# A third PSUM bank for the row maxima, and narrow matrix products packed side by side, in a two-layer attention and feed-forward kernel

## The chip, the core and the metric

The kernel runs on one core of a Trainium2 chip. The metric is the device time of one launch in microseconds (us). Three runs of the kernel before gave 6522.10, 6526.37 and 6527.11 us; their median is 6526.37 us. Engines are named as in the profile: PE is TensorE (PEld its weight loads), DVE VectorE, ACT ScalarE, POOL GpSimd, SP the queue that issues most of the DMAs.

## The reference

There are 16 batch elements of 512 tokens with 256 channels, and for each a context of 1601 tokens. Two layers follow each other:

```python
# layer 0
x = x + cross_attention_16_heads(layernorm(x), ctx)   # head size 16, q and k layer-normed per head, softmax over 1601
x = x + gelu_ffn(layernorm(x))                        # 256 -> 64 -> 1024 -> gelu -> 64 -> 256, low rank
# layer 1
x = x + one_head_attention(layernorm(x), ctx, mask)   # head size 16, scores normalised over the 1601 keys, softmax
x = x + soft_moe(layernorm(x))                        # 64 experts with 32 slots each; softmax over the batch and over the slots
```

The change touches everything up to the soft mixture of experts, which is stage two of the kernel and stays as it is.

## The kernel before

Stage one computes all but the experts. Its main loop runs over 16 batch elements and, in each, over 52 steps: 4 groups of 4 heads by 13 chunks of 128 keys (the last has 65). The step's own work on PE stands in a fixed order:

- four score products (`score_columns`, L789), one per head, into two PSUM banks in turn; ACT turns each into exponentials (L1038);
- four or five pieces of row maxima for the next group (`row_piece`, L767, 401 keys each), into two other banks in turn, the ring; DVE reduces each bank to its maximum (L1193). Transposed maxima and the finished heads (`maxima`, `heads_out`) take their turns in the same ring;
- the weighted values (`weigh_values`, L800): four products of 17 columns that write different 32-partition strips of one bank.

In a step the order is: score, piece, place 0, piece, score, piece, place 1, score, piece, place 2, score, piece, weighted values. At the three places stand the woven steps, which a table of positions (`woven`) spreads over the 52 steps: position 16.67 is place 2 of step 16. They belong to two chains. The head of the next batch element (T transposed input, K keys and values, Q queries, kv1 layer-one keys and values, X transposed heads) fills one bank, `hb`, again and again, and ACT empties it. The tail of the previous batch element fills two banks, `b6` and `b7`: attnT, proj, xT, u1, V1 (eight feed-forward chunks up), U2 (eight down), v2, q1, cq, qaT, s1 (13 score chunks of layer one), pv1, out. Each engine takes its instructions in its own written order and waits on semaphores; a woven step that waits holds up all that stands behind it on its engine. A product that reuses a bank waits until its reader is done (`m_free` for the ring, `h_free` for `hb`, `t_act` and `t_dve` for the tail's banks).

A product in fp32 shows as two MATMUL records. Three products are narrow: kv1 (L740) has 32 output rows, U2 (L842) has 64, and s1 (L903) has 32 rows of contraction that count, padded with zeros to 128. POOL normalises (L644 to L647) and applies the gelu parts (L657 to L665).

Of the kernel before, what the change touches and what calls it, by code (L numbers as in the profile page):

```python
# [12 lines left out]
P = 128  # L13
# [46 lines left out]
def woven():  # L60
# [40 lines left out]
    put(4.0, -1, "attnT", 0)  # L101
    put(4.34, -1, "attnT", 1)
    put(5.34, -1, "proj", 0)
    put(5.67, -1, "proj", 1)
    put(6.34, -1, "res", 1, 0)
    put(6.67, -1, "res", 1, 1)
    for t in range(QT):
        put((6.67, 7.0, 7.34, 7.67)[t], -1, "bns", 1, t)
        put((25.34, 25.7, 26.0, 26.34)[t], -1, "bns", 2, t)
        put((44.0, 44.34, 45.0, 45.34)[t], -1, "bns", 3, t)  # L110
    put(8.0, -1, "lnv", 1)
    put(8.01, -1, "lna", 1)
    put(8.02, -1, "base", 2)
    put(9.67, -1, "xT", 1, 0)
    put(10.0, -1, "xT", 1, 1)
    put(10.34, -1, "u1")
    for f in range(FC):
        put((11.0, 11.34, 11.67, 12.0, 15.9, 16.67, 17.67, 18.67)[f], -1, "V1", f)
        put((11.34, 11.67, 12.67, 13.67, 16.34, 17.34, 18.34, 19.34)[f], -1, "gpre", f)
        put((12.34, 13.34, 14.0, 14.67, 18.0, 19.0, 20.0, 21.0)[f], -1, "gtanh", f)  # L120
        put((12.35, 13.35, 14.01, 14.68, 18.01, 19.01, 20.01, 21.01)[f], -1, "gpost", f)
        put((15.67, 16.34, 17.34, 18.34, 20.0, 21.0, 22.0, 23.0)[f], -1, "U2", f)
    put(23.67, -1, "pT2")
    put(24.34, -1, "v2", 0)
    put(24.67, -1, "v2", 1)
    put(25.0, -1, "res", 2, 0)
    put(25.67, -1, "res", 2, 1)
    put(26.67, -1, "lnv", 2)
    put(26.68, -1, "lna", 2)
    put(26.69, -1, "base", 3)  # L130
    put(28.34, -1, "xT", 2, 0)
    put(28.67, -1, "xT", 2, 1)
    put(29.34, -1, "q1")
    put(0.34, -1, "km")
    put(0.7, -1, "kc")
    put(2.0, -1, "v1")
    put(2.5, -1, "v1e")
    put(3.0, -1, "cov")
    put(3.5, -1, "cove")
    put(30.0, -1, "cq")  # L140
    put(30.67, -1, "cqe")
    put(31.34, -1, "cs")
    put(32.0, -1, "cse")
    put(32.01, -1, "sgp")
    put(33.0, -1, "qs")
    put(33.67, -1, "qaT")
    put(34.34, -1, "q1a")
    for c in range(KC):
        put(35.0 + 0.5 * c, -1, "s1", c)
    for k in range(4):  # L150
        put((36.95, 38.95, 40.95, 41.95)[k], -1, "pv1", k)
    put(42.34, -1, "o1")
    for t in range(QT):
        put((43.0, 43.34, 44.0, 44.34)[t], -1, "out", t)
        put((43.67, 44.0, 44.67, 45.0)[t], -1, "res", 3, t)
    put(45.67, -1, "lnv", 3)
    put(45.68, -1, "lna", 3)
    put(47.67, -1, "xT", 3, 0)
    put(48.0, -1, "xT", 3, 1)
    put(49.0, -1, "st3")  # L160
# [15 lines left out]
    "pT2": ("t_act",), "q1": ("t_mm", "t_act"), "kc": ("kc_ready",), "km": ("km_ready",), "cov": ("t_mm",), "cove": ("t_dve",), "cq": ("t_mm",),  # L176
# [9 lines left out]
def landed(b, label, at):  # L186
# [8 lines left out]
    if name == "ldV":  # L195
        return [(f"va_loaded{label[1] % 2}", 16)]
    return [(n, v) for n, v in {"stV": [("v_stored", 16)], "stkv1": [("kv1_stored", 16)],
                                "ldX": [("xw_loaded", 16), ("kv1_loaded", 16)], "st3": [("x_stored", 48)]}.get(name, [])]


def counted():

    value, at = {}, {}
    for it in range(-2, B + 1):
        for s in range(STEPS):
            for place in WOVEN[s]:
                for of, label in place:
# [67 lines left out]
NLOAD = 17 + 2 * (P // HD) + 4 + 1  # L275
# [15 lines left out]
SETUP_DVE = 41  # L291
# [3 lines left out]
def stage_one(nc, x, ctx_d, mask, w, x3_d, xn_d, xnT_d, ident, psum):  # L295

    with ExitStack() as st:
# [3 lines left out]
        S_BANK, M_BANK, V_BANK, H_BANK, T_BANK = (0, 1), (2, 3), 4, 5, (6, 7)  # L301
# [4 lines left out]
        kv1_d = nc.dram_tensor("kv1_scratch", (B, 2 * A1, NK), F32, kind="Internal").ap()  # L306
# [7 lines left out]
        v2 = sb("v2", [RANK, D])  # L314
# [4 lines left out]
        bkv = sb("bkv", [2 * A1, 1])  # L319
# [22 lines left out]
        kv1s = sb("kv1s", [2 * A1, S])  # L342
# [25 lines left out]
        kmean = sb("kmean", [A1, 1])  # L368
        cov = sb("cov", [A1, A1])
        q1T = sb("q1T", [A1, S])  # L370
        qa = sb("qa", [P, QT, 2 * A1])
        ksum = sb("ksum", [2 * A1, 4, 4])
# [72 lines left out]
        def _(sp):  # L445
# [7 lines left out]
                (v2[:, :], w["L0_ffn_V2"]),  # L453
# [5 lines left out]
                (bkv[0:A1, :], w["L1_xattn_bk"].rearrange("(p a) -> p a", a=1)),  # L459
                (bkv[A1:2 * A1, :], w["L1_xattn_bv"].rearrange("(p a) -> p a", a=1)),  # L460
# [3 lines left out]
            ]  # L464
            for j in range(P // HD):
# [31 lines left out]
            def store_keys_one(b, i):  # L497
                n = min(S, NK - i * S)
                sp.wait_ge(h_free, at("h_free", b, "kv1", i))
                sp.dma_start(kv1_d[b][:, i * S:i * S + n], kv1s[:, 0:n]).then_inc(kv1_stored, 16)  # L500
# [36 lines left out]
            def load_tail(b):  # L537
# [3 lines left out]
                if b >= 1:  # L541
                    sp.wait_ge(h_full, at("h_full", b - 1, "s1", KC - 1))
# [141 lines left out]
        def _(pe):  # L684
# [1124 lines left out]
```

## Time and profile before

| | |
|---|---|
| median of 3 runs | 6526.37 us |
| profiled execution, its own time | 6520.53 us |
| its span | 6518.7 us |
| mean granted clock of TensorE | 0.971 |
| busy in the span: PE, DVE, ACT, POOL | 91%, 56%, 51%, 37% |
| stage one, from the start to the first product of stage two | 4666.78 us |
| main loop, batch elements 1 to 15 (478.08 to 4484 us) | 4005.92 us, 267.1 each |
| the last tail by itself (4484 to 4639 us) | 155 us |

The span goes from the first to the last profiled instruction. PE records are pipelined: the end of a record is modelled and lies after the time at which the next product may start, so the distance between the starts of two records, not their length, says what a product costs. A wait that is shorter than this overhang doesn't show as idle time of PE.

### The profile page before, as it was taken

The page shows a single profiled execution, that of the slowest core. Times are in us where ns is not written, and L with a number is a line of the kernel's source. Part 1 is how long each engine was busy: PE and PEld are TensorE (multiplying, and loading weights), DVE is VectorE, ACT ScalarE, POOL GpSimd, SP SyncE. Part 2 cuts the span into 40 slices and gives each one's busy share as a digit, 9 for nine tenths or more (in the row PEclk, how much of TensorE's full clock was granted, in tenths as well). Part 3 has the DMA queues.
Part 4 walks back from the last instruction along what each step waited for, and adds up shares of the span by engine and source line. Part 5 has one row for each costly group of instructions (what it writes and reads, how often), then busy time and mean ns, then how long its engine had stood idle before and what let it go on. Part 6 is the DMA issues. An engine that isn't in the chain of part 4 may idle for free. (4 is left out here: it accounts for less than half of the span.)

```text
span 6518.7 us, 93097 instructions
## 1 busy us (share of the span) xinstructions
PE 5927.6 (91%) x35613; PEld 2981.1 (46%) x35613; DVE 3677.9 (56%) x6989; ACT 3300.6 (51%) x6257; POOL 2407.3 (37%) x2686
## 2 busy tenths in 40 slices
PE   3789999999999999999999999997599999998999
PEld 1223333333333333333333333322388888886888
DVE  3565656656566565565665656661366666652333
ACT  1366666666666666666666666654222222223332
POOL 3226355363462634636346364443222222220000
PEclk9799999999999999999999999997799999999999
DMA  2441432414324143241332423310356666666553
GB/s 63 78 76 51 79 72 58 83 50 77 69 58 85 49 76 69 61 86 50 74 70 60 84 56 71 62 28 15 127 187 214 221 213 214 209 211 249 211 195 117
DMA packets 417819, 680.30 MB, mean 104 GB/s; under 512 B 61376, under 2 KB 316432, under 8 KB 415072
## 3 DMA queue, kind: packets, MB, share of 16 engines
q1 hardware_dynamic: 307552, 565.29, 34.0%
q10 hardware_dynamic: 109824, 109.07, 5.0%
q8 instruction: 282, 4.62, 0.3%
q14 instruction: 161, 1.32, 0.1%
HBM read 455.04 MB, written 218.39 MB: 103 GB/s over the span
## 5 line engine op out<-in xcount | busy, mean ns | idle before, releaser
L1193 DVE TENSOR_REDUCE mx<-psum 128x1 f32<-128x401 f32 x4096 | 2212.1, 570 | 1612.8 <-PE psum L767 1603.7
L1038 ACT ACTIVATE probs<-psum 128x512 f32<-128x512 f32 (+1 forms) x3328 | 1910.5, 599 | 906.6 <-PE psum L789 903.5
L767 PE MATMUL psum<-kst,qst 96*128 96x401 bf16 x4096 | 1354.9, 343 | 191.9 <-DVE mx L1193 150.9
L789 PE MATMUL psum<-qst,kst 99*128 99x512 bf16 (+1 forms) x3328 | 1284.5, 386 | 49.8 <-ACT probs L1038 44.8
L800 PE MATMUL psum<-probs,vaug 128*17 128x512 f32 x6656 | 885.8, 604 | 0.0
L789 PEld LDWEIGHTS psum<-qst,kst 99*128 99x128 bf16 (+1 forms) x3328 | 328.8, 99 | 1177.1 <-ACT probs L1038 750.4
L767 PEld LDWEIGHTS psum<-kst,qst 96*128 96x128 bf16 x4096 | 402.6, 98 | 961.4 <-DVE mx L1193 756.1
L1486 POOL TENSOR_TENSOR disp<-disp,rz 128x2048 f32<-128x2048 f32 x64 | 294.3, 4599 | 925.4 <-DVE rz L1716 925.4
L1505 PE MATMUL psum<-phi,xT 128*128 128x128 f32 x4096 | 512.2, 280 | 39.2 <-DMA xT<-xnT_scratch 31.9
L1520 PE MATMUL psum<-disp,xnb 128*128 128x128 f32 x4096 | 495.5, 280 | 49.9 <-DMA xnb<-xn_scratch 30.7
L1505 PEld LDWEIGHTS psum<-phi,xT 128*128 128x128 f32 x4096 | 480.4, 193 | 86.9 <-issue 79.2
L1520 PEld LDWEIGHTS psum<-disp,xnb 128*128 128x128 f32 x4096 | 479.9, 196 | 58.5 <-DMA xnb<-xn_scratch 31.1
L644 POOL TENSOR_SCALAR rs<-mv 128x4 f32<-128x4 f32 x48 | 11.1, 231 | 1242.4 <-DVE mv L1245 1242.4
L725 PE MATMUL psum<-wkv,cT 128*128 128x512 f32 (+1 forms) x832 | 406.6, 611 | 12.7 <-ACT sq L1006 7.2
L1749 DVE COPY disp<-psum 128x512 f32<-128x512 f32 x256 | 176.9, 691 | 366.4 <-PE psum L1562 366.3
L1574 PE MATMUL psum<-disp 128*128 128x256 f32 x1536 | 366.6, 380 | 4.6 <-DVE xnb L1766 2.5
L1595 ACT ACTIVATE disp<-psum 128x512 f32<-128x512 f32 x256 | 152.1, 597 | 430.6 <-PE psum L1505 430.3
L1621 ACT ACTIVATE xT<-xT,nm 128x512 f32<-128x512 f32 x256 | 181.0, 708 | 347.7 <-DMA xT<-logit_scratch 338.7
L1723 DVE TENSOR_TENSOR ysb<-psum,be 128x512 f32<-128x512 f32 x128 | 88.5, 691 | 461.7 <-PE psum L1535 450.3
L1627 ACT ACTIVATE slT<-psum 128x512 f32<-128x512 f32 x128 | 76.4, 597 | 435.9 <-PE psum L1520 435.9
L1574 PEld LDWEIGHTS psum<-disp 128*128 128x128 f32 x1536 | 276.0, 190 | 39.6 <-DVE xnb L1766 5.6
L1535 PE MATMUL psum<-we,slT 128*32 128x256 f32 x4096 | 248.6, 383 | 0.0
(190 smaller groups left out, 7527.2 us busy)
## 6 DMA issues: line engine op xcount, KB each, us to landing
xnb<-xn_scratch SPq DMA_DIRECT2D x256, 512.0 KB, 3.8
kst<-k_planes SPq DMA_DIRECT2D x384, 200.1 KB, 8.7
logit_scratch<-disp ACTq DMA_DIRECT2D x64, 1024.0 KB, 5.3
xT<-logit_scratch SPq DMA_DIRECT2D x32, 2048.0 KB, 8.3
k_planes<-pl SPq DMA_DIRECT2D x96, 384.0 KB, 3.2
y_scratch<-ysb ACTq DMA_DIRECT2D x128, 256.0 KB, 5.3
vaug<-v_scratch SPq DMA_DIRECT2D x64, 442.0 KB, 4.3
v_scratch<-vst SPq DMA_DIRECT2D x48, 544.0 KB, 3.1
```

The source lines that it names most:

```text
L725: last = mm(hb[0:m, :], cT[:, n % 2, k, a * P:a * P + m], wkv[:, k, :], start=(k == 0), stop=(k == 1))
L767: mm(to[:, 0:PW], qst[g][0:NP, j, t * P:(t + 1) * P], kst[g][0:NP, j, k0:k0 + PW], start=True, stop=True).then_inc(m_full, 1)
L789: mm(bank[S_BANK[n % 2]][0:m, :], kst[g][0:NR, j, c * P:c * P + m], qst[g][0:NR, j, :], start=True, stop=True).then_inc(s_full, 1)
L800: last = mm(bank[V_BANK][32 * j:32 * j + HV, :], vaug[0:m, g % 2, c, HV * j:HV * (j + 1)], probs[0:m, 4 * (k % 2) + j, :], start=(c == 0), ...
L1038: fn(probs[0:m, 4 * (k % 2) + j, :], bank[S_BANK[j % 2]][0:m, :], ACT.Exp, scale=float(HD) ** 0.5).then_inc(s_exp, 1)
L1193: v.tensor_reduce(mx[:, n % 2, u // 4, u % 4:u % 4 + 1], bank[M_BANK[r % 2]][:, 0:PW], AX.X, ALU.max).then_inc(m_free, 1)
L1486: pool.tensor_tensor(d, d, rz[:, n % 2, None, :].broadcast_to((P, B, SL)), ALU.mult).then_inc(normed, 1)
L1505: last = mm(bank[u % 4][:, a * SL:(a + 1) * SL], xT[:, 4 * q + a, k, t * P:(t + 1) * P], phi[:, k, s * SL:(s + 1) * SL], start=(k == 0), s ...
L1520: last = mm(bank[4 + n % 2][:, (2 * a + h) * SL:(2 * a + h + 1) * SL], xnb[:, a, t, h * P:(h + 1) * P], disp[:, (QT * s + t) % RING, b, :] ...
L1535: last = mm(bank[6 + n % 2][32 * j:32 * j + 32, a * D:(a + 1) * D], slT[:, n % 2, a, k, 32 * j:32 * j + 32], we[:, s % 2, j, k, :], start= ...
L1574: last = mm(bank[4 + t][:, a * D:(a + 1) * D], exT[n % 4][:, t * P:(t + 1) * P], ya[b % 4][:, e, :], start=(e == 0 and a == 0), stop=(e == ...
L1621: fn(d, d, ACT.Exp, bias=nm[:, t, b:b + 1], accum_out=sums[:, b % 4, t, h:h + 1]).then_inc(c_exp, 1)
```

## The change

- The ring of row maxima gets bank 7 as a third bank in steps 0 to 37 and 47 to 51 of every batch element (`LENT`). Each use takes the bank whose last use is the oldest. The order of pieces and scores in a step is as before.
- The tail keeps only bank 6, but for steps 38 to 46, where pv1 and out use bank 7 as before. Its two-bank steps become fill, empty, fill, empty, and their positions in the table move. V1 4 to 7 use `hb`, the bank of the head.
- U2: two chunks at once into the two halves of bank 6 (64 partitions each). The halves are added by v2, whose contraction is now 128 rows, with the weights twice below each other.
- kv1: the 512 tokens are cut in four, and the four products of 128 tokens write four 32-partition strips of `hb`. ACT reads 128 x 128 instead of 32 x 512. The keys' sums then lie in four strips, and a small product with `sel` (the new step km) adds them. The store and the load of `kv1T` are cut to match, and the load is made twice, into partitions 0 to 31 and 64 to 95 (four DMAs instead of one).
- s1: two chunks at once, one from rows 0 to 63 into `hb`, one from rows 64 to 127 into bank 6; the queries `q1a` lie twice, in rows 0 and 64. Seven steps instead of 13.
- There are 7 more loads of weights and 10 more set-up instructions on DVE.

```diff
-    put(4.0, -1, "attnT", 0)
-    put(4.34, -1, "attnT", 1)
+    put(3.0, -1, "attnT", 0)
+    put(3.67, -1, "attnT", 1)
...
-    put(47.67, -1, "xT", 3, 0)
-    put(48.0, -1, "xT", 3, 1)
+    put(49.34, -1, "xT", 3, 0)
+    put(50.0, -1, "xT", 3, 1)
...
+LENT = [s < 38 or s > 46 for s in range(STEPS)]
...
+        free = [m for m in (2, 3, 7) if m != 7 or (LENT[k % STEPS] and k < B * STEPS)]
+        home = min(free, key=lambda m: -1 if last[m] is None else last[m])
...
                 for k in range(2):
-                    last = mm(hb[0:2 * A1, 0:m], w1kv[:, k, :], cT[:, n % 2, k, 0:m], start=(k == 0), stop=(k == 1))
+                    for j in range(-(-m // P)):
+                        w = min(P, m - j * P)
+                        last = mm(hb[32 * j:32 * j + 32, 0:w], w1kv[:, k, :], cT[:, n % 2, k, j * P:j * P + w],
+                                  start=(k == 0), stop=(k == 1), skip_group_check=True)
...
             def ring_bank(use):
-                n = RING[use]
-                if n >= 2:
-                    pe.wait_ge(m_free, n - 1)
-                return bank[M_BANK[n % 2]]
+                home = HOMES[RING[use]]
+                if home[1] is not None:
+                    pe.wait_ge(m_free, home[1] + 1)
+                if len(home) == 3 and home[2] >= 0:
+                    pe.wait_ge(t_dve, at("t_dve", home[2], "res", 3, QT - 1))
+                return bank[home[0]]
...
             def project(b, i):
-                pe.wait_ge(t_act, at("t_act", b, "attnT", 1))
+                if i == 0:
+                    pe.wait_ge(t_act, at("t_act", b, "attnT", 1))
+                else:
+                    pe.wait_ge(t_dve, at("t_dve", b, "res", 1, 0))
...
             def ffn_up(b, f):
-                before = ("u1",) if f < 2 else ("V1", f - 2) if f < 5 else ("V1", f - 1)
-                pe.wait_ge(t_act, at("t_act", b, *before))
-                to = b7 if f in (1, 3) else b6
-                mm(to[:, :], v1[:, f * P:(f + 1) * P], pT[0:RANK, :], start=True, stop=True).then_inc(t_mm, 1)
...
+                if f < 4:
+                    pe.wait_ge(t_act, at("t_act", b, *(("V1", f - 1) if f else ("u1",))))
+                    to, signal = b6, t_mm
+                else:
+                    head_bank(b, "V1", f)
+                    to, signal = hb, h_full
+                mm(to, v1[:, f * P:(f + 1) * P], pT[0:RANK, :], start=True, stop=True).then_inc(signal, 1)
...
-                mm(b7[0:RANK, :], u2[:, f, :], hx[:, f % 4, :], start=(f == 0), stop=(f == FC - 1)).then_inc(t_mm, 1)
+                pe.wait_ge(g_post, at("g_post", b, "gpost", 2 * p + 1))
+                for a in range(2):
+                    last = mm(b6[RANK * a:RANK * a + RANK, :], u2[:, 2 * p + a, :], hx[:, (2 * p + a) % 4, :],
+                              start=(p == 0), stop=(p == FC // 2 - 1), skip_group_check=True)
+                last.then_inc(t_mm, 1)
...
+                mm(hb[0:m, :], kv1T[0:64, c * P:c * P + m], q1a[0:64, :], start=True, stop=True).then_inc(h_full, 1)
+                if c + 1 < KC:
+                    mm(b6[:, :], kv1T[64:P, (c + 1) * P:(c + 2) * P], q1a[64:P, :], start=True,
+                       stop=True).then_inc(t_mm, 1)
```

The row order on PE in steps 16 and 17 of a batch element, before. L842 is a U2 product, L748 the head's X, L836 a V1 product; L789 and L767 are scores and pieces, L800 the weighted values:

```order
L842 MATMUL psum<-hx,u 64x512
L748 MATMUL psum<-ident,kraw 128x128 x4
L789 MATMUL psum<-qst,kst 128x512
L767 MATMUL psum<-kst,qst 128x401
L836 MATMUL psum<-pT,v 128x512
L789 MATMUL psum<-qst,kst 128x512
L767 MATMUL psum<-kst,qst 128x401
L800 MATMUL psum<-probs,vaug 17x512 x4
```

The same place now (U2 is L900, X is L789, V1 is L893; scores L832, pieces L810, weighted values L843):

```order
L900 MATMUL psum<-hx,u 64x512 x2
L789 MATMUL psum<-ident,kraw 128x128 x4
L832 MATMUL psum<-qst,kst 128x512
L810 MATMUL psum<-kst,qst 128x401
L893 MATMUL psum<-pT,v 128x512
L832 MATMUL psum<-qst,kst 128x512
L810 MATMUL psum<-kst,qst 128x401
L843 MATMUL psum<-probs,vaug 17x512 x4
```

U2 is now a pair. V1 stands one score and one piece behind X as before, but it now fills the bank that X has just filled (`hb`), where before it filled bank 6.

PE at the start of layer one's scores, before (s1 is L903, its weighted values pv1 are L914):

```order
L903 MATMUL psum<-g_a,kv1T 128x512
L767 MATMUL psum<-kst,qst 128x401
L789 MATMUL psum<-qst,kst 128x512
L767 MATMUL psum<-kst,qst 128x401
L903 MATMUL psum<-g_a,kv1T 128x512
L789 MATMUL psum<-qst,kst 128x512
L767 MATMUL psum<-kst,qst 128x401
L914 MATMUL psum<-hx,kva 32x512 x4
```

and now (s1 is L967 for the even chunk and L969 for the odd one, pieces L810):

```order
L967 MATMUL psum<-g_a,kv1T 128x512
L969 MATMUL psum<-g_a,kv1T 128x512
L810 MATMUL psum<-kst,qst 128x401
L832 MATMUL psum<-qst,kst 128x512
L810 MATMUL psum<-kst,qst 128x401
L832 MATMUL psum<-qst,kst 128x512
L810 MATMUL psum<-kst,qst 128x401
L832 MATMUL psum<-qst,kst 128x512
```

The chunks now come in pairs with more than a step between pairs, and pv1 no longer follows two instructions behind the last chunk that it needs.

## Rows read from the trace of the kernel before

**Rows 1.** Windows: batch elements 1 to 15, the last tail; busy (x) PE, PEld, DVE, ACT, POOL, clock.

```profile
478.08:4484.00 4005.92, 3770.13 (x18760) 1296.78 (x18756) 2437.19 (x5248) 2554.78 (x4888) 1903.60 (x2347) 1.00 0.31 65
4484.00:4639.00 155.00, 82.85 (x217) 32.32 (x217) 14.19 (x48) 26.80 (x42) 75.04 (x65) 0.62 0.03 10
```

**Rows 2.** Waits from 2095.06 to 2365.20 us, one batch element: total us, times, longest.

```profile
PEld psum L767 <- DVE mx L1193: 44.4, 87, 1.3
...
PE psum L767 <- DVE mx L1193: 8.5, 25, 0.8
...
PE psum L789 <- ACT probs L1038: 2.4, 6, 0.8
...
PE psum L914 <- ACT hx L1083: 1.6, 3, 0.5
```

**Rows 3.** Timeline of PE, a step without woven products: start, us, in brackets idle before.

```profile
2007.17 0.39 PE L789 MATMUL psum<-qst,kst 99*128 99x512 bf16 x1
2007.39 0.51 PE L767 MATMUL psum<-kst,qst 96*128 96x401 bf16 x2
2007.74 0.38 PE L789 MATMUL psum<-qst,kst 99*128 99x512 bf16 x1
2008.40 0.34 PE L767 MATMUL psum<-kst,qst 96*128 96x401 bf16 x1 [0.28 <-DVE mx L1193]
...
2009.43 0.34 PE L767 MATMUL psum<-kst,qst 96*128 96x401 bf16 x1
2009.71 1.05 PE L800 MATMUL psum<-probs,vaug 128*17 128x512 f32 x8
2010.69 0.39 PE L789 MATMUL psum<-qst,kst 99*128 99x512 bf16 x1
```

**Rows 4.** Timeline of DVE, the same step.

```profile
2007.77 0.57 DVE L1193 TENSOR_REDUCE mx<-psum 128x1 f32<-128x401 f32 x1 [0.81 <-PE psum L767]
...
2008.33 2.06 DVE L1193 TENSOR_REDUCE mx<-psum 128x1 f32<-128x401 f32 x4
```

**Rows 5.** Timeline of PE in the last group of heads: steps without pieces.

```profile
4462.07 0.60 PE L789 MATMUL psum<-qst,kst 99*128 99x512 bf16 x2
4463.15 0.88 PE L789 MATMUL psum<-qst,kst 99*128 99x512 bf16 x2 [0.47 <-ACT probs L1038]
...
4464.94 0.60 PE L789 MATMUL psum<-qst,kst 99*128 99x512 bf16 x2
```

**Rows 6.** Timeline of PE around a kv1, and around a U2 and a V1.

```profile
1312.49 1.90 PE L740 MATMUL psum<-cT,w1kv 128*32 128x512 f32 x4
1314.33 0.39 PE L789 MATMUL psum<-qst,kst 99*128 99x512 bf16 x1
...
2455.74 1.07 PE L842 MATMUL psum<-hx,u 128*64 128x512 f32 x2
2456.74 1.12 PE L836 MATMUL psum<-pT,v 64*128 64x512 f32 x2
2457.79 0.39 PE L789 MATMUL psum<-qst,kst 99*128 99x512 bf16 x1
```

**Rows 7.** Timeline of PE around an s1.

```profile
1506.98 1.02 PE L903 MATMUL psum<-g_a,kv1T 128*128 128x512 f32 x2
1507.84 0.38 PE L789 MATMUL psum<-qst,kst 99*128 99x512 bf16 x1
```

**Rows 8.** Timeline of PE and ACT in a step 16: X, then V1.

```profile
2191.68 0.66 PE L748 MATMUL psum<-ident,kraw 128*128 128x128 f32 x4
2192.65 1.12 PE L836 MATMUL psum<-pT,v 64*128 64x512 f32 x2
...
2193.05 0.77 ACT L1031 ACTIVATE pl<-psum,bcol,gcol 128x512 bf16<-128x512 f32 x1
2194.18 0.70 ACT L1059 ACTIVATE hx<-psum,b1c 128x512 f32<-128x512 f32 x1
```

**Rows 9.** Timeline of PE, step 47: the wait for the normalised rows.

```profile
2348.36 0.66 PE L823 MATMUL psum<-ident,xn 128*128 128x128 f32 x4 [0.65 <-POOL xn L647]
```

**Rows 10.** Timeline of DVE, set-up: the wait for the last load of weights.

```profile
30.58 0.98 DVE L1136 CAST hx<-kraw 16x1601 f32<-16x1601 int32 x1 [19.85 <-DMA kraw<-in_mask_BxS_bk]
```

More of the change, by code:

```diff
@@ L141, in woven @@
[L141 to L149, printed above, removed]
+        put((11.34, 12.0, 12.67, 13.34, 16.67, 17.67, 18.36, 20.0)[f], -1, "V1", f)
+        put((11.67, 12.34, 13.0, 13.67, 17.0, 18.0, 19.0, 20.34)[f], -1, "gpre", f)
+        put((12.67, 13.34, 14.0, 14.67, 18.34, 19.34, 20.34, 21.34)[f], -1, "gtanh", f)
@@ new lines, in woven @@
+        put((12.68, 13.35, 14.01, 14.68, 18.35, 19.35, 20.35, 21.35)[f], -1, "gpost", f)
+    for p in range(FC // 2):
+        put((16.34, 18.34, 21.67, 23.67)[p], -1, "U2", p)
+    put(24.34, -1, "pT2")
+    put(25.0, -1, "v2", 0)
+    put(25.34, -1, "res", 2, 0)
+    put(25.67, -1, "v2", 1)
+    put(26.34, -1, "res", 2, 1)
+    put(27.34, -1, "lnv", 2)
+    put(27.35, -1, "lna", 2)
+    put(27.36, -1, "base", 3)
+    put(29.0, -1, "xT", 2, 0)
+    put(29.67, -1, "xT", 2, 1)
+    put(30.34, -1, "q1")
@@ L150, in woven @@
+    put(0.34, -1, "km")
+    put(0.67, -1, "kmr")
+    put(1.0, -1, "kc")
+    put(31.0, -1, "cq")
+    put(31.67, -1, "cqe")
+    put(32.34, -1, "cs")
+    put(33.0, -1, "cse")
+    put(33.01, -1, "sgp")
+    put(34.0, -1, "qs")
+    put(34.67, -1, "qaT")
+    put(35.34, -1, "q1a")
+    for p in range((KC + 1) // 2):
+        put((36.0, 37.0, 38.34, 39.34, 40.67, 41.67, 43.0)[p], -1, "s1", p)
     for k in range(4):
-        put((36.95, 38.95, 40.95, 41.95)[k], -1, "pv1", k)
-    put(42.34, -1, "o1")
+        put((38.0, 40.34, 42.67, 43.67)[k], -1, "pv1", k)
@@ L161, in woven @@
+    put(50.0, -1, "xT", 3, 1)
+    put(50.67, -1, "st3")
     table = [[[] for _ in range(3)] for _ in range(STEPS)]
@@ L464, in _ @@
             ]
+            for j in range(4):
+                loads.append((bkv[32 * j:32 * j + A1, :], w["L1_xattn_bk"].rearrange("(p a) -> p a", a=1)))
+                loads.append((bkv[32 * j + A1:32 * j + 32, :], w["L1_xattn_bv"].rearrange("(p a) -> p a", a=1)))
             for j in range(P // HD):
@@ L856, in layer_one_queries, with keys_mean @@
                 last.then_inc(t_mm, 1)
+            def keys_mean(b):
+                pe.wait_ge(h_free, at("h_free", b, "kv1", 3))
+                if b >= 1:
+                    pe.wait_ge(t_act, at("t_act", b - 1, "xT", 3, 1))
+                mm(b6[:, 0:4], sel[:, :], ksum[:, b % 4, :], start=True, stop=True).then_inc(t_mm, 1)
             def layer_one_tokens(b):
                 pe.wait_ge(kc_ready, at("kc_ready", b, "kc"))
-                if b >= 1:
-                    pe.wait_ge(t_act, at("t_act", b - 1, "xT", 3, 1))
+                pe.wait_ge(t_dve, at("t_dve", b, "res", 1, 1))
                 for c in range(KC):
@@ L1150, in _ @@
                                     ident[32 * j:32 * j + 32, 32 * j + A1:32 * j + A1 + 1]))
+            for j in range(4):
+                for r in (0, 64):
+                    setup(v.tensor_copy(sel[32 * j:32 * j + A1, r:r + A1],
+                                        ident[32 * j:32 * j + A1, 32 * j:32 * j + A1]))
             setup(v.tensor_scalar(bq[:, :], bq[:, :], 1.0 / A1, None, ALU.mult))
```

263 lines of the change are left out of this document (142 added, 121 removed).

## The prediction

> **What bounds the kernel now.** I read the windows by stage first. Batch elements 1 to 15 take 4005.92 us, 267.1 each, at a granted clock of 1.00, and PE is busy 94% of it, DVE 61%, ACT 64% [rows 1]. So PE's own work and the waits inside its row of instructions set the time, and neither DVE nor ACT is full. This stretch is 61% of the span and the change lies in it; stage two isn't touched.
>
> The waits say what holds PE. In one batch element of 270.14 us 87 weight loads of pieces wait for DVE to empty a ring bank, and 25 of these leave PE idle, 8.5 us in all; the exponentials leave it idle 2.4 us, pv1 1.6 us [rows 2]. Idle time understates a wait. In the plain step the piece at 2008.40 could have started at 2007.96 (the score at 2007.74 and the 0.22 us that a score takes), so it waited 0.44 us, while the row shows 0.28 [rows 3]. With 0.17 us more for each of the 25, and half of that for the 62 shorter waits, the ring costs 8.5 + 4.2 + 5.2 = 17.9 us a batch element. I take 17. Steps 38 to 46, which keep two banks, hold about 3 of it, since their waits are of the same kind; 14 us are open to the third bank.
>
> The plain step lasts 3.52 us from score to score [rows 3], with waits of about 0.7: four scores of 0.22, five pieces of 0.17 and 0.98 for the weighted values with 0.1 in front make 2.8. DVE needs 0.57 us for a piece and 0.51 when they queue [rows 4], 2.6 for five. It stands idle 0.81 us while PE does the weighted values and then keeps PE waiting: two banks are too short a queue between them.
>
> **The change part by part**, per batch element.
>
> *kv1.* A full block takes 1312.49 to 1314.33, 1.84 us [rows 6]. Afterwards there are 16 records of 128 columns. If four strips run together as in the weighted values, where eight records of 512 columns take 0.98 us, the four waves cost about 0.11 us each: 0.45, and 0.1 to leave. That saves 1.25. If they don't run together, 16 by 0.11 is 1.76 and nothing is saved. I take the first, since L800 is the same form: 3 blocks, 3.75 us.
>
> *U2.* One takes 1.00 us (2455.74 to 2456.74), and about 0.1 in front, where a change of tile shape costs 0.28 instead of 0.17 after a piece (2009.43 to 2009.71) [rows 3, 6]. Eight cost 8.8. A pair side by side costs 1.03 and the 0.1: 4.5. Saved 4.3; one after the other, a pair costs 1.9 and 0.5 is left. I take 4.3.
>
> *s1.* Now 0.86 us each (1506.98 to 1507.84) [rows 7], 13 of them 11.2. A product of 64 rows takes 1.05 (V1, 2456.74 to 2457.79) [rows 6] and 0.1 in front. Two on different rows of the array into different banks are in no row of this trace. If they run together, seven steps cost 8.0 and 3.2 is saved. If one follows the other, a pair costs 1.05 + 0.86 + 0.1 = 2.0 and the seven 13.1, a loss of 1.9. The nearest row is L800, four products on different columns that do run together, so I take 3.2 and keep 1.9 of loss as the other end. The Trainium skill, "TensorEngine Tiling (Array Packing)", section Key Properties, says that tiles operate independently and can load weights and multiply in parallel. By it the saving holds; by a serial array the whole would be 77 us slower. No run here shows it for rows.
>
> *v2, qaT, km.* v2 loses its 64-row form and its changes of shape, 0.5 saved; qaT 0.2 saved; km adds one small product, 0.25. Between nothing and 1; I take 0.4.
>
> *pv1.* It stood two instructions behind its last s1 and waits three times, 1.6 us idle [rows 2]. It now stands over half a step behind. I take 1.6.
>
> *The ring.* With three banks the piece at 2008.40 goes at once. The next waits move to the scores: S2 needs the exponential of S0, 0.38 us to fill, 0.60 to read, 0.06 to come back, so about 1.06 after S0 against 0.96 in the row of work; S3 is late by about 0.2. I get 3.1 us for the plain step. Its floor is the last group of heads, which has no pieces and still takes 2.87 (4462.07 to 4464.94), with 0.47 idle for ACT [rows 5]. So of 0.7 us of waits 0.4 goes, at most 0.65. In steps where ACT has a long woven read between two exponentials (for X twice 0.77 us [rows 8]), next to nothing goes. Over all I take half of the 14: 7.0, between 2 and 12.
>
> *New waits.* (a) V1 4 to 7 share `hb` with the head. In step 16 X starts at 2191.68 and ACT has read it at 2193.82, 2.1 us later; V1 follows 0.97 us after X [rows 8]. It will wait 1.2 us there, about 0.65 in step 17, and T and K behind V1 about 0.8: 2.65. Behind V1 on PE wait a score, a piece and the weighted values, so DVE and ACT run dry with it. (b) proj 1 waits for the residual of proj 0 one place ahead: DVE is through 1.7 us after the last piece's start (0.4 to fill, 0.6 to reduce, 0.7 for the residual), PE arrives after 0.6: 1.1, less the 0.4 that the ring lost there. v2 1 has the same wait, in a step where the ring already loses it. (c) xT 3 waits for POOL already, 0.65 idle [rows 9]; its two steps get shorter and POOL's chain doesn't: 0.4. (d) Halves of attnT, xT and V1 0 to 3 on the single bank: mostly two places apart, 0.5. (e) On SP the last store of a tail now goes out just before the loads of the next maxima, two steps closer than now: 0.5. Sum 4.8, I take 5; between 2.5 and 10. Without the spacing of two places, (d) alone would cost some 0.8 us at each of ten places.
>
> Sum: 3.75 + 4.3 + 3.2 + 0.4 + 1.6 + 7.0 - 5 = 15.25 us; times 15 is 229. Batch element 0 runs without a tail and gains by the ring alone, 7.5. Against this stand 5 us in set-up (DVE waits for the last load at 30.58 [rows 10]; seven more issues and ten more instructions lie before it or behind it) and 5 in the last tail by itself, where nothing hides the single bank [rows 1]. 226 us less: 6520.53 - 226 = 6294. The median of the runs is 5.8 above the profiled execution: 6300.
>
> **The rivals.**
> - *Rows of the array don't run in parallel* (12%). 5.1 us more for each of 15: 6377. Against it speaks only the likeness to L800.
> - *The ring's waits move to ACT* (8%). Two banks of scores are as short a queue as the ring was, and rows 5 show ACT making PE wait where there are no pieces. If only 1 us of the 14 is won: 6390. The Trainium skill, same page, section PSUM Bottleneck, speaks against the change in this sense: faster products don't speed the reading of PSUM. Here s1 and V1 are read at the same 0.70 us as before; only kv1's read gets shorter.
> - *More than forecast* (7%). The ring wins 12 and the new waits cost 3: 6195.
> - *The tail's single bank costs more than all gains* (5%). About 17 products now stand behind a read that they didn't depend on: attnT 1, proj 1, three xT, three V1, v2 1, and eight in `hb`. Each may have to wait for an exponential (0.60) and its own read (0.70) behind the fill (0.3), less 0.4 of PE work between. From 1.2 us each the gains of 20 us are gone; at 1.3 it is 22 a batch element and the time 6556. For it: the table puts several such pairs one place apart. Against it: most are two places apart, with over a microsecond of PE work between.
>
> **How the numbers follow.** The forecast, 6300, has 68%, with a range of its own of 6240 to 6365 from the ends of ring and waits. The range for 8 in 10 takes in most of the serial rows and of ACT as the bound, and on the low side the better case: 6190 to 6425. The kernel's runs lie within 0.1% of each other, so 0.2% (13 us) tells a change. All cases but the last are faster by far: 93%. Within 0.2% needs the waits to meet the gains just so: 2%. Slower: 5%.
>
> **What would show it.** The window of batch elements 1 to 15 should fall from 267 to about 252 us each. In the plain step pieces stop waiting for DVE and the step lasts about 3.1 us; DVE's idle time before L1193 shrinks. In steps 38 to 46 the ring's waits stay. The four records of a U2 pair and of an s1 pair should start two by two, and a full kv1 should take 0.6 us. V1 in steps 16 and 17 should wait for ACT by about 1 us. If the starts of an s1 pair lie 0.43 us apart one by one, the first rival holds; if scores wait for L1038's like over 10 us a batch element, the second; if PE's idle time is spread over tail products behind reads, the last.

## The result, and the profile after

| | before | after |
|---|---|---|
| median of the runs (us) | 6526.65 | 6450.32 |
| lowest and highest (us) | 6522.10 to 6527.11 | 6442.85 to 6458.40 |
| span of the profiled run (us) | 6518.7 | 6456.4 |
| mean granted clock of TensorE | 0.971 | 0.955 |

The changed kernel takes 0.9885 of the time, with a 95% interval of 0.9868 to 0.9902: 76 us less. The forecast was 226 us less, and the time lies above the range of 6190 to 6425. The sign was right, the size was not: 150 us of the gain are missing.

The two stretches that answer to [rows 1], in the windows after; columns as there (PE, PEld, DVE, ACT, POOL busy, clock, DMA share, GB/s). The second one reaches to the first product of stage two, which before came 182.8 us behind the main loop:

```profile
465.90:4413.50 3947.60, 3635.88 (x19294) 1293.86 (x19290) 2389.14 (x5264) 2531.83 (x4888) 1909.21 (x2347) 0.98 0.32 67
4413.50:4606.00 192.50, 84.58 (x219) 31.03 (x219) 14.55 (x49) 26.57 (x42) 75.16 (x65) 0.53 0.17 67
```

A batch element of the main loop takes 3947.60 / 15 = 263.2 us, against 267.1 before and 252 in the forecast. PE is busy 134 us less in all, yet the stretch is only 58 us shorter: the work went, and waits came. The span divides like this: before the second batch element 12.2 us less (478.08 against 465.90; 3.0 of it in set-up, 9.2 in batch element 0), batch elements 1 to 15 58.3 less, the rest 8.2 more (the last tail with its single bank 9.9 more, where 5 were forecast). Together 62.3, the difference of the spans.

I then gave every product on PE its own cost (the distance to the next start that the same kind of product has when nothing holds it) and called the rest waiting, step by step, averaged over 13 batch elements of the main loop. Before: 241.6 us of own work and 28.1 of waits. After: 226.8 and 39.6. (The sums, 269.7 and 266.4, lie above the 267.1 and 263.2 of the windows, since the last batch element, which is shorter, is not among the 13.) Own work fell by 14.8 us a batch element, more than the 11.65 forecast; waits rose by 11.5, though the ring and pv1 gave back about 8.5.

**The products.** A kv1, a U2 pair and an s1 pair on the timeline of PE, to be held against [rows 6, 7]:

```profile
1134.90 0.64 PE L780 MATMUL psum<-cT,w1kv 128*32 128x128 f32 x16
1135.47 0.39 PE L832 MATMUL psum<-qst,kst 99*128 99x512 bf16 x1
...
2158.20 1.08 PE L900 MATMUL psum<-hx,u 128*64 128x512 f32 x4
2159.21 0.66 PE L789 MATMUL psum<-ident,kraw 128*128 128x128 f32 x4
...
2161.40 1.12 PE L893 MATMUL psum<-pT,v 64*128 64x512 f32 x2 [1.15 <-ACT pl L1101]
...
2263.90 0.69 PE L967 MATMUL psum<-g_a,kv1T 64*128 64x512 f32 x1
2263.91 0.69 PE L969 MATMUL psum<-g_a,kv1T 64*128 64x512 f32 x1
2264.43 0.59 PE L967 MATMUL psum<-g_a,kv1T 64*128 64x512 f32 x1
2264.44 0.59 PE L969 MATMUL psum<-g_a,kv1T 64*128 64x512 f32 x1
2264.96 0.34 PE L810 MATMUL psum<-kst,qst 96*128 96x401 bf16 x1
```

kv1 takes 0.57 us instead of 1.84 (forecast 0.6). A U2 pair takes 1.01, as long as a single one before. The four records of an s1 pair start two by two, 0.01 us apart, and the pair takes 1.06: products on different rows of the array run side by side. This agrees with what the Trainium skill, "TensorEngine Tiling (Array Packing)", section Key Properties, says of tiles. The row of V1 also shows the forecast wait behind X: 1.15 us idle there, 1.2 forecast.

**The ring.** A plain step on PE and DVE, to be held against [rows 3, 4]:

```profile
2247.39 0.39 PE L832 MATMUL psum<-qst,kst 99*128 99x512 bf16 x1
2247.61 0.51 PE L810 MATMUL psum<-kst,qst 96*128 96x401 bf16 x2
...
2249.52 1.05 PE L843 MATMUL psum<-probs,vaug 128*17 128x512 f32 x8
2250.51 0.39 PE L832 MATMUL psum<-qst,kst 99*128 99x512 bf16 x1
```

```profile
2247.99 0.58 DVE L1272 TENSOR_REDUCE mx<-psum 128x1 f32<-128x401 f32 x1 [0.81 <-PE psum L810]
...
2248.55 2.01 DVE L1272 TENSOR_REDUCE mx<-psum 128x1 f32<-128x401 f32 x4
```

The step lasts 3.12 us instead of 3.52 (forecast 3.1) and no piece waits for DVE. DVE does the same work and is idle 0.81 us as before. I had forecast that its idle time would shrink, and in this step it doesn't. The waits of one batch element, 2069.70 to 2336.20 us, answer to [rows 2]:

```profile
PEld psum L832 <- ACT probs L1108: 57.8, 82, 1.7
...
PEld psum L810 <- DVE mx L1272: 19.5, 39, 1.1
```

The loads of pieces that wait for DVE fell from 87 to 39. In the step-by-step account pieces wait 6.2 us for DVE instead of 16.05, and scores wait 6.8 us for ACT instead of 3.8. Net 6.8 us, where 7.0 were forecast.

**What PE waits for** over the whole span (us in total, times, longest). Before, then after:

```profile
PE psum L767 <- DVE mx L1193: 150.9, 462, 0.9
...
PE psum L823 <- POOL xn L647: 37.9, 19, 8.9
```

```profile
PE psum L877 <- POOL xn L682: 90.8, 33, 8.6
...
PE psum L832 <- DMA qst<-nT: 52.0, 14, 5.6
PE psum L810 <- DVE mx L1272: 39.7, 134, 1.2
```

Two rows carry most of what is missing. The wait of xT for POOL grew from 37.9 to 90.8 us. The wait of the first score of step 39 for its row maxima (`qst<-nT`), which before stood there once (4.1 us, in batch element 0), now comes 14 times and takes 52.0.

*Step 39.* The loads on SP and the score that waits, in a batch element of after (an entry groups the issues of a line; the second fence is PE). The last fence gives the packets of nT, as the DMA view of this stretch has them (KB each, median us from issue to landing):

```profile
1980.93 2.68 SPq L557 DMA_DIRECT2D kst<-k_planes  x6
...
1989.27 2.77 SPq L559 DMA_DIRECT2D qst<-q_planes  x6
1997.60 1.84 SPq L592 DMA_DIRECT2D qst<-nT  x3
```

```profile
2004.51 1.05 PE L843 MATMUL psum<-probs,vaug 128*17 128x512 f32 x8
2009.65 0.61 PE L832 MATMUL psum<-qst,kst 99*128 99x512 bf16 x1 [4.10 <-DMA qst<-nT]
```

```profile
qst<-nT SPq DMA_DIRECT2D x3, 4.0 KB, 10.3
```

The same place before:

```profile
1740.91 3.16 SPq L525 DMA_DIRECT2D kst<-k_planes  x6
...
1762.23 1.84 SPq L557 DMA_DIRECT2D qst<-nT  x3
```

```profile
1769.92 1.05 PE L800 MATMUL psum<-probs,vaug 128*17 128x512 f32 x8
1770.90 0.39 PE L789 MATMUL psum<-qst,kst 99*128 99x512 bf16 x1
```

```profile
qst<-nT SPq DMA_DIRECT2D x3, 4.0 KB, 3.2
```

Ahead of nT stand the 24 loads of two stacks of keys and queries, 3.2 MB, which need 26.7 us from the first issue to the last landing (2007.67), some 120 GB/s. Before, nT was issued 21.3 us behind the first of them, landed 25.6 us behind it, and PE got to the score at 30.0. Now PE is quicker between the two places: nT is issued after 16.7 us, behind the same queue of data, and its three loads land at 2007.90, 2008.36 and 2009.61 (28.7), right behind the last of the 24, while PE wants the score at 24.6 (2005.5). Most of the 5.4 us that PE is quicker here is the change's own doing: three pairs of s1 (1.06 us each) stand between the two places where eight single ones (0.86 each) stood, and one pv1 instead of two. The shorter way of PE ran into a transfer that had 4 us to spare.

*Step 29.* POOL ahead of xT 2. After (L649 to L654 is the key norm of block 4, `kn` 4; L679 to L682 the normalisation, `lna` 2), and before (L614 to L619, L644 to L647):

```profile
2218.67 0.22 POOL L649 TENSOR_TENSOR root<-rstd 128x16 f32<-128x16 f32 x1 [5.28 <-DVE rstd L1267]
...
2222.26 0.62 POOL L654 TENSOR_TENSOR kraw<-kraw,rstd 128x256 f32<-128x256 f32 x1
2222.96 0.23 POOL L679 TENSOR_SCALAR rs<-mv 128x4 f32<-128x4 f32 x1
...
2224.43 4.85 POOL L682 TENSOR_SCALAR xn<-xw,mv,rs 128x256 f32<-128x256 f32 x4
```

```profile
2252.04 0.23 POOL L644 TENSOR_SCALAR rs<-mv 128x4 f32<-128x4 f32 x1 [5.19 <-DVE mv L1245]
...
2253.51 4.84 POOL L647 TENSOR_SCALAR xn<-xw,mv,rs 128x256 f32<-128x256 f32 x4
...
2260.77 0.22 POOL L614 TENSOR_TENSOR root<-rstd 128x16 f32<-128x16 f32 x1
```

The tail's positions moved, and `lna` 2 went from 26.68 to 27.35, behind `kn` 4. Its 4.3 us of small instructions (2218.67 to 2222.96) now come first; the normalised rows that xT 2 needs wait for them, and xT 2 stood 3.14 us idle in this element.

*The clock.* Windows of after around step 39 (before, behind and well behind the wait); columns as above:

```profile
2004.00:2009.90 5.90, 1.80 (x13) 0.36 (x11) 1.06 (x2) 1.99 (x4) 0.00 (x0) 0.85 1.11 145
2009.90:2016.50 6.60, 6.60 (x23) 1.69 (x22) 2.79 (x5) 3.44 (x6) 0.00 (x0) 0.62 1.05 124
2016.50:2024.00 7.50, 6.93 (x39) 1.86 (x37) 4.39 (x10) 4.97 (x9) 0.00 (x0) 1.00 0.48 96
```

PE idles 4.1 us, and behind that the granted clock is 0.62 over 6.6 us in which PE is always busy: the lower level, 1.2 GHz, for most of it. A score record there lasts 0.61 us instead of 0.39. Over the main loop the records of the granted clock stand at 0.5 for 38 us before and 195 us after. Half of the difference, 79 us, is the most that it can cost, about 5 us a batch element; that is an estimate from these records.

### The profile page after: what moved, and what is told of

Read it like the earlier page. It is cut to its first block and busy times, and to the rows that moved or that the text cites. A ratio compares the mean times of both kernels' runs of the same rounds, so it can differ in the third digit from the quotient of the medians.

```text
span 6456.4 us, 94456 instructions
## 1 busy us (share of the span) xinstructions
PE 5788.5 (90%) x36221; PEld 2983.0 (46%) x36221; DVE 3624.8 (56%) x7015; ACT 3274.9 (51%) x6257; POOL 2413.6 (37%) x2686
## 5 line engine op out<-in xcount | busy, mean ns | idle before, releaser
L1272 DVE TENSOR_REDUCE mx<-psum 128x1 f32<-128x401 f32 x4096 | 2169.3, 569 | 1591.6 <-PE psum L810 1583.2
L810 PE MATMUL psum<-kst,qst 96*128 96x401 bf16 x4096 | 1362.3, 346 | 90.6 <-DVE mx L1272 39.7
L832 PE MATMUL psum<-qst,kst 99*128 99x512 bf16 (+1 forms) x3328 | 1312.3, 395 | 119.1 <-ACT probs L1108 59.8
L832 PEld LDWEIGHTS psum<-qst,kst 99*128 99x128 bf16 (+1 forms) x3328 | 332.5, 100 | 1355.5 <-ACT probs L1108 903.1
L843 PE MATMUL psum<-probs,vaug 128*17 128x512 f32 x6656 | 894.8, 610 | 0.0
L810 PEld LDWEIGHTS psum<-kst,qst 96*128 96x128 bf16 x4096 | 407.4, 100 | 592.4 <-DVE mx L1272 339.8
L679 POOL TENSOR_SCALAR rs<-mv 128x4 f32<-128x4 f32 x48 | 11.2, 232 | 1203.9 <-DVE mv L1324 1202.7
```

The costliest lines, as they stand in the source:

```text
L810: mm(to[:, 0:PW], qst[g][0:NP, j, t * P:(t + 1) * P], kst[g][0:NP, j, k0:k0 + PW], start=True, stop=True).then_inc(m_full, 1)
L832: mm(bank[S_BANK[n % 2]][0:m, :], kst[g][0:NR, j, c * P:c * P + m], qst[g][0:NR, j, :], start=True, stop=True).then_inc(s_full, 1)
L843: last = mm(bank[V_BANK][32 * j:32 * j + HV, :], vaug[0:m, g % 2, c, HV * j:HV * (j + 1)], probs[0:m, 4 * (k % 2) + j, :], start=(c == 0), ...
L1272: v.tensor_reduce(mx[:, n % 2, u // 4, u % 4:u % 4 + 1], bank[HOMES[r][0]][:, 0:PW], AX.X, ALU.max).then_inc(m_free, 1)
```

## The experiments

All were timed beside the kernel before, whose median there was 6527.3 us (e1 to e4) and 6524.3 (the others). "The changed kernel" is the one of this document.

**The stack loads behind the row maxima** (e1_stacks_later).

```diff
-    put(head["X", 4, 0] + 2.2, 1, "ldS", 1)
+    put(38.4, 1, "ldS", 1)
```

> Base is the changed kernel (6450 us), with one edit: the loads of group 1's stacks (ldS 1, 12 DMAs) are issued at position 38.4, behind the loads of the row maxima, instead of 33.7, ahead of them. Theory A (the forecast gains are there, and waits at three places take them back: the maxima's loads in step 39, POOL in steps 29 and 49): step 39 loses its 5.4 us of waits and slow clock down to about 1, so 4 to 5 us in each of 15 batch elements: 6375 to 6395 us. Theory B (PE has no slack to give: whichever wait goes, scores or pieces wait instead): within 15 us of 6450.

Measured 6352.52 us, 0.9734 of before (0.9719 to 0.9748): 98 us less than the changed kernel, more than expected. Its SP row now has the row maxima first:

```profile
1951.59 2.77 SPq L592 DMA_DIRECT2D qst<-nT  x3
1954.40 2.93 SPq L557 DMA_DIRECT2D kst<-k_planes  x6
```

The 52.0 us row is gone from PE's waits, step 39 falls from 9.32 to 4.61 us, and a batch element from 266.5 to 259.4. So one transfer cost two thirds of what was missing, the clock behind it included: the half-clock records of the main loop fall from 195 to 65 us, so up to 65 of the 98 us can be the clock's.

**The key norm behind the normalisation** (e2_kn_behind).

```diff
-        put(head[done] + 0.72, 1, "kn", n)
+        put(head[done] + (1.82 if n == 4 else 0.72), 1, "kn", n)
```

> Base is the changed kernel (6450 us), with one edit: the scaling of the last block's keys on POOL (kn 4) stands behind the normalisation lna 2 instead of ahead of it, as it stood in the kernel before. Theory A: POOL is through with xn about 3.7 us sooner, the wait of xT 2 in step 29 (4.9 us with what follows it) falls to under 1: 6380 to 6400 us. Theory B: within 15 us of 6450. A third way: X 4 0 in step 31 now waits for kn 4; then little is won and the wait shows there.

Measured 6412.17 us, 0.9818 (0.98 to 0.9835): 38 us less than the changed kernel; the expectation was 12 us too hopeful. Step 29 falls from 8.62 to 5.30 us, but step 37 rises from 5.76 to 8.08, because there a piece waits for loads of `q_planes`: a part of the gain ran into the next transfer. Step 39 in turn falls to 6.89, since PE gets there later.

**Both** (e3_both).

> Both edits of the two runs before together. Theory A: the two gains add up, 8 to 9 us a batch element, 6310 to 6335 us, and the granted clock rises from 0.957 towards the 0.971 of the kernel before, because the long idle stretches of PE go. If only one of them counts, or the clock is what counts and one spell stays: 6370 to 6390. Theory B: about 6450.

Measured 6321.38 us, 0.9684 (0.9669 to 0.9698), 129 us less than the changed kernel, as expected. A batch element takes 258.0 us, own work 226.8 as in the changed kernel, waits 31.1. The half-clock records add up to 58 us instead of 195.

**The late loads in the kernel before** (e12_before_stacks_later), the control: the edit of e1 alone, in the kernel without the change.

> The kernel before, with the loads of its second stack of keys at 38.4 instead of 33.7, as in the edit that made the changed kernel 98 us faster. Theory: there the row maxima land 4.3 us before the score that needs them, so nothing waits for them and moving the loads wins nothing: 6520 to 6532, ratio 0.998 to 1.002. Rival: the loads cost time by themselves (the queues, or the memory traffic) in both kernels: 6430 to 6500.

Measured 6516.22 us, 0.9989 (0.9979 to 0.9998), 4 us under the expected range. At most 0.2%, where the same edit gives the changed kernel 1.5%; and from batch element 1's weighted values to the last ones it takes 3997.4 us against 3995.8, so the main loop gained nothing. The loads cost next to nothing by themselves; it is the change that made them late.

**The third bank taken away** from the changed kernel (e4_two_banks) and from e3 (e8_two_banks_untangled).

```diff
-LENT = [s < 38 or s > 46 for s in range(STEPS)]
+LENT = [False for s in range(STEPS)]
...
-                if k == 0:
+                if k == 0 and any(LENT):
                     pe.wait_ge(m_free, lent_until(b) + 1)
```

> The changed kernel without the third bank for the ring (LENT false in all steps), all else as it is. It measures the ring's share. Theory A: the ring's own worth is about 7 us a batch element (105 in all), but longer steps give the late loads time, so that 3 to 4 of the 5 us in step 39 come back: 6480 to 6510 us. Rival (the ring's waits have only moved to ACT and the third bank is worth nothing): 6440 to 6465. If the third bank alone carried the whole gain: over 6520.

> Base is the run with both edits (6321 us), without the third bank for the ring. With the late loads out of the way the ring's own worth shows: in the traces DVE's and ACT's waits of PE fell together by 6.8 us a batch element. Theory A: 100 to 120 us slower, 6420 to 6440. If its worth is only the 62 us that the same edit showed on the changed kernel: 6380 to 6390, and the late loads didn't hide part of it.

Measured 6512.70 us (0.9975, 0.9966 to 0.9984) and 6445.27 us (0.9876, 0.9861 to 0.989). The second hunk drops pv1's wait for the lent bank. The third bank is thus worth 62 us in the changed kernel, 3 us beyond the expectation, and 124 in e3, more than expected there. Both numbers hold about 13 us of set-up (the first weighted values start at 263 and 264 us in these two kernels, at 249 to 256 in the other kernels with the change). The ring explains 8 of them: in set-up the 64 pieces of the first group stand behind one another, and from the first piece to the first score it is 37.2 us with three banks (the changed kernel and e3) and 45.3 with two (e4, e8 and the kernel before). The other 5 lie in the start of the first piece, which waits for loads of `q_planes`; it varies from 203.4 to 210.3 us between kernels whose ring in set-up is the same, and that stays open. In the profiled runs of e8 and e3, 13 us more lie behind the last weighted values of the main loop, where their ring does nothing; these are open too. From the start of batch element 1's weighted values to the last ones it is 2.5 us a batch element in the changed kernel (3976.2 against 3938.1) and 6.3 in e3 (3911.2 against 3817.3). PE's waits for DVE, in e8 and then in e3:

```profile
PE psum L810 <- DVE mx L1272: 175.0, 562, 0.9
```

```profile
PE psum L810 <- DVE mx L1272: 43.2, 147, 1.2
```

The ring's waits go in both kernels alike. In the changed kernel PE used the time to arrive at step 39 earlier and wait there longer: with two banks `qst<-nT` costs 14.8 us, with three 52.0, and step 39 takes 5.72 and 9.32 us. Step 29, with its wait for POOL, takes 6.41 and 8.62.

**The later xT 2 and xT 3** (e5_xt_later; on e3; the chain behind xT 2 up to qaT moves along).

```diff
-    put(29.0, -1, "xT", 2, 0)
-    put(29.67, -1, "xT", 2, 1)
+    put(29.67, -1, "xT", 2, 0)
+    put(30.34, -1, "xT", 2, 1)
...
-    put(49.34, -1, "xT", 3, 0)
-    put(50.0, -1, "xT", 3, 1)
+    put(50.0, -1, "xT", 3, 0)
+    put(50.67, -1, "xT", 3, 1)
```

> Base is the run with both edits (stack loads and kn 4, 6321 us). Here xT 2 and xT 3, with what follows them up to qaT and the last store, stand two thirds of a step later. Theory A (the waits for POOL in steps 29 and 49, 1.6 and 1.9 us, are a matter of the table's positions): both fall to under 0.5, 2.5 to 3.5 us a batch element, 6270 to 6290 us. Theory B (PE has no slack, something else waits instead): within 10 us of 6321. Beside it the end of the tail comes closer to the next batch element's start, which can bring back up to 1 us in steps 0 to 3.

Measured 6301.59 us, 0.9658 (0.9643 to 0.9672), 20 us less than e3 where at least 31 were expected. The waits in steps 29 and 49 go, but step 32 now waits 1.23 us, 1.2 more than in e3, and the head's X 4 0 in step 31 stands 1.5 us idle for `kn` 4 on POOL in every batch element from 1 to 14 (in e3 only the one wait of 6.3 in set-up is there):

```profile
PE psum L792 <- POOL kraw L654: 27.1, 15, 6.3
```

PE, no longer held in step 29, gets to X before POOL is through with the key norm that e2 had put behind the normalisation. Steps 29 to 36 together are 2.1 us *longer* than in e3; what is won comes from steps 49 and 50 (2.6) and 37 (1.3). xT 3 moved alone was not run.

**The second halves of proj and v2 one place later** (e6_halves_apart; on e3).

```diff
-    put(5.67, -1, "proj", 1)
+    put(6.0, -1, "proj", 1)
...
-    put(25.67, -1, "v2", 1)
+    put(26.0, -1, "v2", 1)
```

> Base is the run with both edits (6321 us). Here proj 1 and v2 1 stand two places behind the residual that they wait for (positions 6.0 and 26.0 instead of 5.67 and 25.67). Theory A (the single bank costs a wait where two halves are one place apart, 1.4 us each, and none where they are two apart): 2.0 to 2.8 us a batch element, 6280 to 6292. Theory B: the stall only moves, to DVE's late pieces in the same steps: within 10 us of 6321.

Measured 6294.41 us, 0.9649 (0.9635 to 0.9664), 27 us less than e3; the expectation was 2 us off at its upper end. Steps 5 and 6 fall together from 9.83 to 8.38 us, 25 and 26 from 11.74 to 10.38.

**V1 away from X** (e7_v1_apart; on e3).

```diff
+    head["X", 1, 1] += 0.45
...
-        put((11.34, 12.0, 12.67, 13.34, 16.67, 17.67, 18.36, 20.0)[f], -1, "V1", f)
-        put((11.67, 12.34, 13.0, 13.67, 17.0, 18.0, 19.0, 20.34)[f], -1, "gpre", f)
+        put((11.34, 12.0, 12.67, 13.34, 17.0, 18.36, 19.34, 20.0)[f], -1, "V1", f)
+        put((11.67, 12.34, 13.0, 13.67, 17.34, 18.67, 19.67, 20.34)[f], -1, "gpre", f)
```

> Base is the run with both edits (6321 us). Here V1 4, 5 and 6 stand at 17.0, 18.36 and 19.34, and X 1 1 half a step later, so that V1 no longer follows X in hb within a step. The waits of V1 for ACT in steps 16 and 17 (1.2 and 0.65 us), of the pieces behind them (0.85) and of T 3 1 (0.5) should fall to about 1 in all. Theory A: 1.5 to 2.5 us a batch element, 6285 to 6300. Theory B: within 10 us of 6321.

Measured 6397.36 us, 0.9809 (0.979 to 0.9828): 76 us *more* than e3, a clear miss. Steps 16 and 17 did get 3.1 us shorter, but step 19 went from 4.67 to 11.85. ACT, PE and POOL there (lines lie one higher than in the changed kernel: L1139 is the tanh of the gelu, L1135 the read of V1, L764 K, L698 the last instruction of `gpre`):

```profile
2138.78 0.63 ACT L1139 ACTIVATE gt<-gt 128x512 f32<-128x512 f32 x1 [3.83 <-POOL gt L698]
2139.32 0.67 ACT L1135 ACTIVATE hx<-psum,b1c 128x512 f32<-128x512 f32 x1
```

```profile
2140.04 3.67 PE L764 MATMUL psum<-wkv,cT 128*128 128x512 f32 x4 [4.00 <-ACT hx L1135]
```

```profile
2135.66 1.04 POOL L696 TENSOR_TENSOR gt<-hx 128x512 f32<-128x512 f32 x1
...
2137.49 1.26 POOL L698 TENSOR_TENSOR gt<-gt,hx 128x512 f32<-128x512 f32 x1
```

POOL has the gelu of chunk 5 ready late; the tanh waits for it on ACT; the read of V1 6 stands behind the tanh; K needs the bank that this read empties. My expectation had followed V1's own bank and not what stood in front of its read.

**The tanh behind the read** (e11_tanh_later; on e7).

```diff
-        put((12.67, 13.34, 14.0, 14.67, 18.34, 19.34, 20.34, 21.34)[f], -1, "gtanh", f)
-        put((12.68, 13.35, 14.01, 14.68, 18.35, 19.35, 20.35, 21.35)[f], -1, "gpost", f)
+        put((12.67, 13.34, 14.0, 14.67, 18.34, 20.0, 20.34, 21.34)[f], -1, "gtanh", f)
+        put((12.68, 13.35, 14.01, 14.68, 18.35, 20.01, 20.35, 21.35)[f], -1, "gpost", f)
```

> The kernel with V1 4 to 6 moved away from X (6397), with one edit more: the tanh of chunk 5 and what follows it on POOL stand at 20.0 instead of 19.34, so on ACT behind the read of V1 6. Theory: that kernel lost its time because ACT stood 3.8 us before this tanh (POOL, 12 instructions behind each other, finishes the input of chunk 5 only then), the read of V1 6 stood behind it, and K waited for the read, 4.7 us a batch element. With the read ahead of the tanh K goes at once; ACT then still waits about 1 us for POOL. 15 times 4.7 and the slow-clock stretch behind it (about 1) are 85 less: 6310, between 6285 and 6335. Rival: POOL itself is late in these steps, and the wait only moves to the exponentials behind the tanh or to U2: 6360 to 6400.

Measured 6309.91 us, 0.9672 (0.9654 to 0.969), as expected: 87 us come back with two numbers. K's wait for the read, in e7 and then here:

```profile
PE psum L764 <- ACT hx L1135: 56.0, 14, 4.0
```

```profile
PE psum L764 <- ACT hx L1135: 4.0, 14, 0.3
```

**e5 and e6 together** (e10_x_and_halves; on e3).

> The two edits that won 20 and 27 us one by one (the later xT with its chain, and the second halves of proj and v2 one place later) together, on top of the later stack loads and the later key norm. Theory: they take away waits in different steps (29 and 49, and 5 and 25), so the gains add: 6321 - 20 - 27 = 6274, between 6265 and 6285. Rival: the chain through POOL from v2's residual to xT 2 absorbs what v2 wins, and the second half of proj only moves a wait: 6290 to 6300.

Measured 6282.17 us, 0.9628 (0.9611 to 0.9644): 39 us less than e3, inside the expected range, 8 short of the plain sum. Step 32 still waits 1.45 us, and X 4 0 in step 31 stands 1.47 idle for `kn` 4.

**All edits** (e13_all).

> All edits on top of one another: later stack loads, later key norm, later xT chain, second halves of proj and v2 one place later, V1 4 to 6 away from X, and the tanh of chunk 5 behind the read of V1 6. If the gains add: 6274 (the first five) less the 3.1 us that steps 16 and 17 won, less about 1 that steps 18 to 21 lose, times 15: 6243, between 6225 and 6270. If POOL is what is late in steps 18 to 21, no better than 6274 and up to 6320.

Measured 6243.02 us, 0.957 (0.9553 to 0.9588), the point of the expectation. That it is met so well is in part luck: the expectation started from 6274 for the first edits together, which measured 6282, and the last two gave 39 us where 31 were expected. It is 207 us faster than the changed kernel and 281 faster than the one before, and beats both. Its main loop:

```profile
457.90:4206.00 3748.10, 3575.57 (x19294) 1275.89 (x19290) 2384.95 (x5264) 2524.30 (x4888) 1904.01 (x2347) 0.99 0.33 70
```

That is 249.9 us a batch element, with the products and the banks of the change as they were: only positions in the table differ.

## Why the prediction was wrong

Per batch element of the main loop, in us gained:

| term | forecast | measured |
|---|---|---|
| own work of PE (kv1, U2, s1, v2, qaT, km) | 11.65 | 14.8 |
| pv1 | 1.6 | 1.7 |
| ring, less what moves to ACT | 7.0 | 6.8 |
| new waits, slower clock included | -5 | about -20 |
| sum | 15.25 | 3.2 |

The measured column is that of the step-by-step account; its last term is what is left, and the windows of the whole loop give 3.9 for the sum. About 19 of the 20 us have a place: V1 with T and K behind it 2.75, proj 1 and v2 1 2.87, step 29 4.95, step 37 1.70, step 39 5.37, and step 49 about 1.8 more than before.

**Right.** kv1, U2 and s1 came out as forecast or better, and the rival of serial rows fell. The ring gave 6.8 against 7.0, and the plain step 3.12 us against 3.1, so ACT didn't take its place; e8 against e3 gives 6.3 by taking the bank away. Of the new waits, those that I named by following one bank came out well: V1 behind X 1.22 in step 16 and 0.65 in step 17 (forecast 1.2 and 0.65), T and K behind V1 0.88 (0.8), proj 1 1.42 and v2 1 1.45 (1.1 each; the sum held 0.7 and nothing, because the ring's own wait there was set against them). The single bank did not cost 1.2 us at 17 products. Steps 38 to 46 keep their waits for DVE.

**The step that failed is the term "New waits"**, put at 5 us where about 20 were measured: in its points (e) and (c) and in what the list left out.
- (e) looked at the row maxima's loads, but only at those of the end of a batch element and at what stands ahead of them in SP's row of issues, and put them at 0.5 us. The loads that came late are those for step 39, which no point names, and what held them was the data of 24 loads issued long before. Step 39 waits 5.37 us in place of almost nothing, 3.24 of it idle for nT. The margin stood in the trace of before (about 4 us), and the change takes 5.4 us away between the issue of the first of these loads and the score, most of it by s1 steps that the forecast itself had shortened and moved. e1 and e12 show it from both sides: 98 us in the changed kernel, about 8 in the other and none of them in its main loop.
- (c) put xT 3 at 0.4 and didn't name xT 2. Step 29 waits 4.95 us (3.36 for POOL), step 49 waits 2.48 (1.88 for POOL). The part in step 29 that comes from `kn` 4 standing ahead was a change of order on POOL, to be seen before the run; I looked at the order of PE and not of POOL. e2 shows 38 us of it, and 31 more on top of e1.
- Not in the list: the loads of `q_planes` in steps 36 and 37 (1.70 us in step 37), and the clock. I gave no price to idle stretches of PE beyond their own length, and behind those of 4 us in step 39 stands a stretch at half the clock; over a batch element all such stretches cost up to 5 us more than before. That the clock's part is so large is worked out from its records; no run here changes the clock alone.

e1 and e2 together give 129 of the missing 150 us. That e3 ends only 21 us above the forecast is partly luck: its new waits are still 11.6 us a batch element, 6.6 more than forecast (step 37 waits 2.4, steps 29 and 49 1.6 and 1.9), and the own work that came out 3.15 better than forecast hides half of that. Most of the gain of the change was thus there, and it was swallowed at two places behind PE's faster stretches. That is shown by e3, and by e8 against e4: the same bank is worth 6.3 us a batch element once the way is free, and 2.5 before.

The set-up came out better than forecast: scores start 3.0 us earlier (242.50 against 245.46), where 5 more were forecast. The first piece does start 5.1 us later (205.30 against 200.20), but as this start varies by 7 us between kernels with the same ring in set-up, that confirms nothing. From there to the first score the third bank wins 8.1 us (37.2 against 45.3). The forecast had left the ring out of the set-up.

One sum in the forecast is off, with nothing resting on it: four U2 pairs at 1.9 us, one product behind the other, would take 7.6, which saves 1.2 and not 0.5.

## What to carry to other kernels

When a change shortens PE's way between two places, list what else runs between them (a transfer, a chain on POOL) with its slack, and compare each slack with the shortening: whatever has less becomes the bound. For a load, the slack counts from the data in flight ahead of it, not from its place in the issuing queue. And compare the order of all engines: a position that moves for one engine's sake reorders the others, and a read may stand behind an instruction that waits for something else (e7 and e11, 87 us).

## What the runs showed of the hardware that I had not expected

- Three loads of 4 KB needed a median of 10.3 us from issue to landing behind 24 loads of stacks, and 3.2 us when they were issued 4.6 us later behind the same ones. Both times the third of them landed after the last of the 24 (by 1.9 and 0.5 us).
- After an idle stretch of PE of 4.1 us the granted clock was 0.62 over the next 6.6 us and 1.00 in the 7.5 us behind them. If all that PE did there went by the clock, it would have taken 4.1 us at the full one, so the wait of 4.1 us cost up to 2.5 more behind it: an estimate from these records.
- Products on different rows of the array into different banks started 0.01 us apart and took 1.06 us a pair. A single product of 64 rows (V1) took 1.05, one of the full 128 rows 0.86.
- The 64 pieces of the set-up, one 401-column product each, took 30.1 us from the first start to the last with three banks between PE and DVE, and 37.3 with two, at a granted clock of 0.50.
